# The samples of a tile are transposed one step earlier, ahead of that step's last attention product

## The reference

```python
x = x + deform_conv(group_norm(x))          # offsets by a 3x3 conv; 9 taps, each sampled bilinearly
t = tokens(x)                               # 8 x 3136 x 128
t = t + causal_attention(layer_norm(t))     # one head of 128
t = t + expert_ffn(layer_norm(t))           # 64 experts; each takes its 8 best tokens of an image
```

## Time and profile before

| | |
|---|---|
| time, median of 3 runs | 2709.12 us (2708.4 to 2709.32) |
| profiled execution | 2707.96 us, span 2706.1 us |
| mean granted clock of PE | 0.977 |
| PE busy | 2536.2 us, 94% of the span |
| DVE, ACT, POOL busy | 1884.7, 1777.3, 1771.1 us |
| chain that ended last, by engine | PE 71%, DVE 8%, ACT 8%, POOL 6% |

### The profile page before, as it was taken

One profiled execution on the slowest core, in us unless ns is written; L12 is line 12 of the kernel. 1 busy time (PEld: TensorE's weight loads), 2 busy tenths in 40 slices (PEclk: granted clock), 3 DMA queues, 4 the chain that ended last, 5 costly groups with the idle time before them and its releaser, 6 DMA issues.

```text
span 2706.1 us, 53906 instructions
## 1 busy us (share of the span) xinstructions
PE 2536.2 (94%) x19262; PEld 2035.9 (75%) x19262; DVE 1884.7 (70%) x7300; ACT 1777.3 (66%) x4144; POOL 1771.1 (65%) x1831
## 2 busy tenths in 40 slices
PE   4688999999999999999999999999999999899797
PEld 3466787788877887788878887788878887787664
DVE  4456776886678776886678767876688767765435
ACT  3455667776777767776677767677777767775430
POOL 4777776777667775777667776777677776760010
PEclk8799999999999999999999999999999999999899
DMA  6355433653356433653356434643355433542499
GB/s 190 111 160 136 118 114 113 165 140 114 104 160 151 116 114 115 155 140 113 104 157 153 118 113 121 158 132 113 98 170 156 114 111 101 130 100 102 150 333 394
DMA packets 218150, 382.64 MB, mean 141 GB/s; under 512 B 43785, under 2 KB 128713, under 8 KB 216987
## 3 DMA queue, kind: packets, MB, share of 16 engines
q0 software_dynamic: 88992, 250.76, 32.9%
q1 hardware_dynamic: 126299, 113.98, 14.2%
q10 hardware_dynamic: 2592, 14.45, 1.3%
HBM read 316.92 MB, written 62.13 MB: 140 GB/s over the span
## 4 chain that ended last, share of the span: by engine, by line
PE 71%; DVE 8%; ACT 8%; POOL 6%; issue 3%; DMA 3%; SPq 0%; DVEq 0%; ACTq 0%; POOLq 0%
PE bank_o L1307 17%; PE bank_r L1284 17%; PE bank_r L1266 11%; PE bank_r L1293 9%; POOL shared L640 6%; PE bank_r L1258 5%; ACT shared L677 4%; DVE shared L946 2%; PE bank_r L1189 2%; PE bank_r L1168 1%; ACT stages L696 1%; DVE res L1554 1%; DVE res L1111 1%; ACT res L778 1%; PE bank_r L1281 1%
## 5 line engine op out<-in xcount | busy, mean ns | idle before, releaser
L640 POOL DMA_INDIRECT shared<-pair_table,idx x1800 | 1750.6, 973 | 665.8 <-issue 536.8
L1307 PEld LDWEIGHTS bank_o<-res,stages 128*128 128x128 f32 x4800 | 583.8, 192 | 122.5 <-ACT stages L696 66.9
L1307 PE MATMUL bank_o<-res,stages 128*128 128x128 f32 x4800 | 612.5, 277 | 37.7 <-ACT stages L696 37.7
L946 DVE SCALAR_TENSOR_TENSOR shared<-shared,wb 128x128 f32<-128x128 f32 x1800 | 514.0, 347 | 173.0 <-ACT shared L677 172.1
L696 ACT ACTIVATE stages<-bank_r 128x512 f32<-128x512 f32 (+2 forms) x704 | 369.5, 546 | 395.2 <-PE bank_r L1293 393.6
L677 ACT ACTIVATE shared<-shared,wa 128x128 f32<-128x128 f32 x1800 | 561.1, 391 | 66.9 <-DMA shared<-pair_table,idx 65.8
L958 DVE CUSTOM_DVE_ANT_0 res<-bank_r,mask 128x512 f32<-128x512 f32 (+2 forms) x704 | 427.2, 623 | 237.0 <-PE bank_r L1284 218.2
L1284 PE MATMUL bank_r<-res,stages 128*128 128x512 f32 (+3 forms) x1344 | 584.8, 552 | 0.7 <-ACT stages L719 0.3
L1293 PE MATMUL bank_r<-ident,res 128*128 128x128 f32 x2504 | 367.0, 273 | 4.1 <-ACT res L778 3.9
L1266 PE MATMUL bank_r<-stages 128*128 128x128 f32 x2400 | 336.0, 277 | 0.0
L778 ACT ACTIVATE res<-res,nmax 128x1664 f32<-128x1664 f32 (+23 forms) x200 | 325.2, 1626 | 14.7 <-DVE nmax L1076 13.0
(11 more groups left out here) (196 smaller groups left out, 2492.7 us busy)
## 6 DMA issues: line engine op xcount, KB each, us to landing
shared<-pair_table,idx POOLq DMA_INDIRECT x1800
pair_table<-res SPq DMA_DIRECT2D x112, 256.0 KB
shared<-in_dram SPq DMA_DIRECT2D x26, 1024.0 KB, 15.7
res<-in_dram SPq DMA_DIRECT2D x48, 256.0 KB
t_dram<-t SPq DMA_DIRECT2D x48, 256.0 KB
shared<-in_dram SPq DMA_DIRECT2D x7, 1568.0 KB
stages<-t_dram POOLq DMA_DIRECT2D x8, 832.0 KB, 7.4
pm_dram<-res SPq DMA_DIRECT2D x8, 800.0 KB, 7.2
```

Source lines behind the costliest of these rows:

```text
L640: pool.indirect_dma_start(g[t % RING][:, n, :], None, pair_table[b % 2], bass.IndirectOffsetOnAxis(ap=idx[:, b % 2, i * TAPS + n:i * TAPS ...
L946: last = dve.scalar_tensor_tensor(first, g[t % RING][:, n, C:], wb[:, b % 2, i * TAPS + n:i * TAPS + n + 1], first, ALU.mult, ALU.add)
L1307: last = pe.matmul(attn_ps, prob_t[q % 3][:, n * P:(n + 1) * P], vals[:, slot(tb, at), :], start=(at == 0), stop=(at == ti))
```

## The change

The nine transposes of a tile's samples leave the head of its own step. Those of tile 0 stand ahead of the loop. Those of tile s+1 stand in step s: where the attention of the step has two chunks or more, behind the rounds and ahead of the last attention product; where it has fewer, ahead of the rounds. The order of the banks is changed in the same way: the three sample banks of tile s+1 now come ahead of place L of step s (and of place M where there are fewer than two chunks). The programs of the other engines are as before.

```diff
@@ ring_order
+    order += [("smp", 0, p) for p in range(PIECES)]
     for step in range(END):
         ts, v = step - LAG_S, step - LAG_V
-        if step < ALL:
-            order += [("smp", step, p) for p in range(PIECES)]
+        next_samples = [("smp", step + 1, p) for p in range(PIECES) if step + 1 < ALL]
...
         order += [("prob", v, c) for c in range(min(chunks_in(v), 2))]
+        order += next_samples if chunks_in(v) < 2 else []
         for c in inner_rounds(step):
...
             order += misc_at(step, "M") if c == 1 else []
+        order += next_samples if chunks_in(v) >= 2 else []
         order += misc_at(step, "L")
@@ PE's program
+            def turn_samples(t):
+
+                if t >= ALL:
+                    return
+                for p in range(PIECES):
+                    use = ("smp", t, p)
+                    after(sampled, PIECES * t + p + 1)
+                    free_ring(use)
+                    for n in range(3):
+                        last = pe.transpose(ring_bank(use)[:, n * P:(n + 1) * P], g[t % RING][:, 3 * p + n, 0:C], ident[:])
+                    last.then_inc(smp_tp, 1)
+
+            turn_samples(0)
             for step in range(END):
...
-                if step < ALL:
-                    for p in range(PIECES):
-                        turn_samples(p)
                 for c in range(min(chunks_in(ts), 3)):
                     scores(c)
...
                 rounds = inner_rounds(step)
+                if chunks_in(v) < 2:
+                    turn_samples(step + 1)
                 for c in rounds:
...
+                if chunks_in(v) >= 2:
+                    turn_samples(step + 1)
                 if rounds.stop - 1 < chunks_in(v):
                     attend(rounds.stop - 1)
                 for use in misc_at(step, "L"):
```

More of the change, by code:

```diff
@@ L1250, in _ @@
                 b, i = image_of(step)
[L1252 to L1259, removed]
                 def products(p):
```

## The result

The changed kernel takes 2758.93 us (median of 4 runs, 2756.06 to 2761.17) against 2708.76 before: a ratio of 1.0184, with an interval of 1.0169 to 1.0199. It is slower by 50 us, where 39 were forecast. The profiled execution took 2757.55 us, span 2755.8.

The account below looks back on a forecast made before the run. PE was taken to bound a steady image. Six middle images at +5.1 (6.1 + 0.6 + 0.3 − 1.9) give +30.8, image 0 +6.3, image 7 +1.6: +38.7 us, told as 2748 us, range 2713 to 2765.

Parts of the forecast that it names:

- The loss at E: Values or logits (place E) wait for a bank until ACT copies the first sample piece after exp: 6.1 us an image.
- The smaller ones: Four lesser borders at place E, worked out from 0.33 to 0.75 us, taken at 0.5 each: 2.0 us an image.
- The queries: Where L is the query, the next step's first score waits for its later copy: 0.6 us an image, bounds 0 and 0.98.
- What is left of the gain: Middle images: 1.9 of 2.89 us kept at the attention waits, and +0.3 for small places at steps 6 to 8.
- The 0.88 of step 8: PE's wait before the keys of step 8, filled by the transposes but counted as eaten at steps 6 to 8.
- the mechanism named: At steps 6 to 8 PE meets the bank of the previous conv product, which DVE frees late.
- Image 0: Delays before tile 16 absorbed; later sample waits and E's waits cost +6.3 us, bounds 0 and about 12.
- the work that now follows the wait: Image 0, steps 16 to 21: attention product and L now follow the sample wait, about 0.75 × 6 = 4.5 us.
- Image 7: E costs 6.1 us, filled attention waits give −4.4 to −4.9: net +1.6, bounds −4 and +6.
- The covers: Rival: the transposes fill the four waits of each steady image and nothing is late behind them; 2681.6 us, chance 0.08.
- Only ACT is late: Rival: E's bank is free in time and only late copies delay products; +3.2 us, 2712 us, chance 0.08.
- The clock: Rival: new waits lower PE's granted clock by one per cent over 7 images, 21 us; 2769 us, chance 0.08.

Follow-up runs that it names:

- the copies first: The full change, with ACT copying the three sample pieces ahead of the exponential in every step: 2698.05 us, ratio 0.9945.
- the banks alone: PE's program of the kernel before, with only the order of the banks taken from the change: 2718.68 us, ratio 1.0030.
- first experiment: The changed kernel with the banks handed out in the order of before, place L ahead of the sample banks: 2731.35 us, ratio 1.0070.
- the four steps: The kernel before, with transposes moved only in steps 8, 10, 12 and 13 of images 1 to 7, banks as before: 2695.94 us, ratio 0.9940.

## Why the prediction was right, and by how much it was short

The direction, the mechanism of the middle images and the range held; the size was 11 us short: 7.6 of them in the six middle images, 2.2 in image 0 and 1.9 in image 7. Point by point, with the change of each interval from a tile's first product to the next tile's first product in image 3, worked out from the starts in the two traces:

- **The loss at E.** The borders of steps 99, 75, 78 and 80 cost 0.75, 1.06, 1.18 and 1.24 us, where 0.76, 0.96, 1.19 and 1.2 were worked out. The smaller ones, steps 76, 90, 95 and 96, taken at 0.5 each, cost 0.90, 0.99, 0.33 and 0.63: this term, 2.85 in place of 2.0, is the one that was mis-sized. Step 76 had been worked out at 0.75 and still went into the sum at 0.5. At step 90 two pieces of work stand at L, so that the third score, too, has the first sample piece seven uses back. The trace shows the score waiting for the first piece and the logits for the second:

```profile
1174.52 0.70 PE L1290 MATMUL bank_r<-res,stages 128*128 128x256 f32 x2 [0.36 <-ACT res L684]
...
1175.15 0.20 PEld L1204 LDWEIGHTS bank_r<-stages,gate_t 128*64 128x64 f32 x4 [0.33 <-ACT stages L684]
```

  The sum at E is 7.1 us an image in place of 6.1. The experiments with the old banks and with the copies first show its cause twice over.
- **The queries.** Step 81 waits 0.69 us, and its interval grew by 0.62, as forecast (0.6).
- **What is left of the gain.** The intervals of tiles 81 to 88 changed by +0.72, +0.26, −0.93, +0.78, −1.22, +0.05, −0.49 and −0.93: −1.76 together, and +0.33 in steps 15 and 16 behind them. Forecast were −1.9 and +0.3. The 0.88 of step 8 counted as eaten at steps 6 to 8 was indeed won (−0.93) and eaten (+0.72 and +0.26), but not by the mechanism named, so that part of the agreement is luck. The offset product of step 7 waited 0.08 us for DVE in the change, and 1.8 only with the banks alone. Instead step 7's logits waited 0.34 us for ACT's copy of L's own output: the transposes of the samples used to stand between the two and now stand ahead of both. An image: 7.1 + 0.6 − 1.76 + 0.33 + 0.1 at step 1 = 6.4, forecast 5.1.
- **Image 0.** 8.5 in place of 6.3. As forecast, all delays up to tile 16 were absorbed (the first product of tile 16 starts 0.15 us later than before, after up to 9.2 us at tile 11). Tiles 16 to 21 then lose 6.6, where 4.5 and a part of the 1.8 at E stood for them. PE's waits in image 0 behind that, from 248.4 us on:

```profile
PE bank_r L1259 <- DVE shared L948: 7.0, 14, 1.6
```

  Before it was 3.6 us there, 9.9 less the 6.3 at tile 16. The six intervals grew by 2.55, 0.67, 0.89, 0.98, 1.51 and 0.00. The first holds something that the sum did not have, a fall of the clock in image 0. Below are the interval after tile 16's first product and the slow stretch in it, then the same interval with the old order of the banks (first experiment):

```profile
248.45:262.64 14.19, 12.65 (x77) 10.00 (x76) 11.65 (x44) 8.45 (x21) 10.84 (x12) 0.88 0.46 139
256.60:260.01 3.41, 3.41 (x12) 2.40 (x11) 3.05 (x9) 1.44 (x2) 2.60 (x3) 0.50 0.36 96
```

```profile
249.66:262.18 12.52, 10.98 (x77) 8.88 (x76) 10.65 (x43) 8.45 (x21) 9.77 (x10) 1.00 0.45 140
```

  From 256.60 to 260.01 us the granted clock was 0.50, the lower of its two levels (1.2 GHz), and the same 77 matmuls kept PE busy 1.67 us longer than at 1.00. Just before, PE had stood 0.88, 0.33 and 0.33 us before the transposes, waiting for DVE. With the old order of the banks it waited 0.88, 0.34 and 0.32 us there and the clock stayed at 1.00, so why it fell is open. With that order the five intervals grew by 0.89, 0.67, 0.89, 0.65 and 0.88, 4.0 together: the work that now follows the wait, forecast at 0.75 × 6 = 4.5, was sized well. The rest of the 6.6 are the 1.67 of the clock and 1.0 at E of steps 20 and 21. E of steps 24 and 25 adds 1.8, so E cost 2.8 where 1.8 was forecast.
- **Image 7.** 3.5 in place of 1.6. The attention waits fell from 8.0 to 3.9 us, 4.1 where −4.4 to −4.9 were forecast, and the keys of step 12 wait 1.3 us for DVE, behind a wait that the transposes had filled:

```profile
PE bank_o L1313 <- ACT stages L698: 3.9, 3, 2.0
...
PE bank_r L1187 <- DVE res L1064: 1.3, 1, 1.3
```

  The granted clock was 0.99 before and after.
- **The rivals.** The covers do work, as the four steps show (−14 us), but not for nothing behind them. "Only ACT is late" falls with the first experiment: the banks alone decide over 28 of the 50 us. The clock was 1.00 in the middle images, as before; over all of image 0 it was 0.88 where it had been 0.90.

The Trainium skill's rule on a gap that repeats on the saturated engine ("Perfetto Trace Analysis", section "Optimization Strategy") reads such gaps as a sign that PSUM can be short. It fits what came: eight gaps an image at one place of the order, for want of a PSUM bank. More banks, which no run here tried, are not the only way out, since an earlier copy took the gaps away with the same seven.

## What to carry to other kernels

When outputs share a ring of buffers, moving one writer moves the owner of every later buffer: for each, look up who now stands one round back and when its reader gets to it, in the reader's own order. A filler is worth moving only to the steps in which the engine waits; in the others it pushes back what others wait for, here the work at L on which ACT's whole next step hangs. And the order of the copies on the draining engine can be the cheaper edit: short copies ahead of a long exponential freed the banks, and no kernel tried here became slower by it.

## What the runs showed of the hardware that was not expected

A wait in the middle of PE's stream lengthens its interval by more than the idle time that is shown for it. At the border to step 100 the trace of the change shows a wait of 0.79 us before the values, and the interval grew by 1.06. The rows of PE and of its weight loads (PEld) at this border account for it, first before and then after:

```profile
1264.10 2.74 PE L1284 MATMUL bank_r<-res,stages 128*128 128x512 f32 x6
...
1266.25 0.19 PEld L1189 LDWEIGHTS bank_r<-wv_t,res 128*128 128x128 f32 x1 [0.24 <-issue]
...
1266.67 1.05 PE L1189 MATMUL bank_r<-wv_t,res 128*128 128x128 f32 x8
```

```profile
1290.74 2.74 PE L1290 MATMUL bank_r<-res,stages 128*128 128x512 f32 x6
...
1294.27 0.97 PEld L1191 LDWEIGHTS bank_r<-wv_t,res 128*128 128x128 f32 x8 [1.62 <-ACT res L684]
...
1294.27 1.16 PE L1191 MATMUL bank_r<-wv_t,res 128*128 128x128 f32 x8 [0.79 <-ACT res L684]
```

Before, the first weights went in at 1266.25, during the last score, and the first matmul ran at 1266.67; after, load and matmul start together at 1294.27, and from there to the next product it takes 1.00 us where it took 0.89. That is 0.11 of the difference. The other 0.17 comes from how the profile draws a matmul: the scores are drawn up to 1266.84, but the values had started at 1266.67. Behind a wait nothing overlaps that modelled end, and it counts as busy time. 0.79 + 0.11 + 0.17 are the 1.06, within rounding. The Trainium skill, "TensorE: Matmul & The Clock Gate", section "Architectural detail: the array is 16× 32×32, not 1× 128×128", says that PE's queue can pull weight loads ahead of matmuls in flight. The rows agree for the kernel before; in those after, the load did not pass the wait ahead of it.

Over image 3, PE's busy time grew by 3.1 us (296.95 to 300.08) for the same work, and its idle time by 3.2: half of the loss is not shown as waiting. How much of the 3.1 is slower starts and how much only drawn ends was worked out for this one border alone.
